# A bounds limit on the row gathers of a two-stage mixture-of-experts kernel, with four small clears per stage

## The reference

```
x = x + cross_attention(norm(x), ctx, wq, wk, wv, wo)        # own keys beside 1024 context rows
x = x + moe0(norm(x))    # 8 experts, 2 of them per token, inner width 256
x = x + memory_attention(norm(x), ctx, mask)
x = x + moe1(norm(x))    # 32 experts, 8 of them per token, inner width 192
moe: out[t] = sum over chosen experts e of w[t, e] * (silu(x[t] @ wgate[e]) * (x[t] @ wup[e])) @ wdown[e]
```

## Time and profile before

| what | value |
|---|---|
| median of 3 runs | 943.73 us (940.0 to 945.9) |
| the profiled execution, its own time | 939.34 us |
| its span | 937.6 us |
| TensorE / VectorE / ScalarE / GpSimd busy | 85% / 60% / 55% / 46% of the span |
| packets of q1 / q0, share of 16 DMA engines | 30.5% / 24.4% |
| bytes moved by DMA | 143.74 MB |
| moe0, from its first gather to its last scatter | about 282 to 383 us |
| moe1, likewise | about 575 to 912 us |

### The profile page before, as it was taken

The page is one execution under the profiler, slowest core; times in us unless marked ns, Lnnn a source line. Parts: engine busy times, 40 slices in busy tenths (PEclk is TensorE's granted clock), DMA queues, the critical chain, the costliest instruction groups (busy, mean ns, idle before and its releaser), DMA issues.

```text
span 937.6 us, 19263 instructions
## 1 busy us (share of the span) xinstructions
PE 796.3 (85%) x5266; PEld 437.7 (47%) x5267; DVE 559.9 (60%) x1596; ACT 516.6 (55%) x780; POOL 433.0 (46%) x355
## 2 busy tenths in 40 slices
PE   4999999999848999966888735999889899999995
PEld 2444455555425544433443414555555455555552
DVE  5553445555564555685676625576557575667475
ACT  6533234455445776333544523786777787778760
POOL 3882000200014676130075662467776666667862
PEclk9999999999968999998899876999999999999998
DMA  8562200201116696790120102898899897998777
GB/s 287 180 217 98 77 34 23 46 24 35 34 26 207 181 253 147 213 315 7 53 69 26 48 24 67 219 261 251 202 253 262 234 303 192 250 223 260 143 112 276
DMA packets 85842, 143.74 MB, mean 153 GB/s; under 512 B 19462, under 2 KB 36102, under 8 KB 85793
## 3 DMA queue, kind: packets, MB, share of 16 engines
q1 hardware_dynamic: 58880, 93.49, 30.5%
q0 software_dynamic: 24320, 49.45, 24.4%
q10 hardware_dynamic: 2592, 0.19, 0.2%
HBM read 106.25 MB, written 41.28 MB: 157 GB/s over the span
## 4 chain that ended last, share of the span: by engine, by line
PE 49%; issue 13%; DMA 12%; DVE 11%; ACT 6%; DVEq 2%; ACTq 2%; another core or an unknown queue 2%; POOL 1%; SPq 1%; POOLq 0%
PE pst L194 38%; PE pst L1368 4%; DMA mid<-moe_normalised_rows,row_no 3%; DMA x_rows<-mid,row_no 2%; PE pst L515 2%; DMA big<-in_L_ffn_wo_dram 2%; DMA xT<-moe_normalised_rows,row_no 2%; PE pst L1341 2%; DVE big L1247 1%; ACT mid L1431 1%; DMA x_rows<-xT,row_no 1%; PE pst L1423 1%; DVE mid L1520 1%; ACT big L1240 1%
## 5 line engine op out<-in xcount | busy, mean ns | idle before, releaser
L194 PE MATMUL pst<-big,mid 128*128 (+1 forms) x1392 | 272.1, 346 | 19.4 <-ACT mid L1431 13.1
L1056 POOL DMA_INDIRECT moe_tokens_of_experts<-token_no,small x70 | 73.3, 1047 | 271.3 <-DVE small L1141 253.7
L194 PEld LDWEIGHTS pst<-big,mid 128*128 128x128 f16 x1392 | 132.9, 98 | 122.1 <-issue 29.0
L1368 PE MATMUL pst<-big,mid 128*128 x520 | 128.9, 380 | 0.1
L1431 ACT ACTIVATE mid<-pst 128x1024 f16<-128x1024 f16 x100 | 102.5, 1025 | 29.7 <-PE pst L1341 19.9
L1622 POOL DMA_INDIRECT x_rows<-mid,row_no x48 | 90.9, 1894 | 48.8 <-DMA x_rows<-xT,row_no 22.5
L1622 POOL DMA_INDIRECT x_rows<-xT,row_no x46 | 87.7, 1906 | 52.3 <-DMA x_rows<-mid,row_no 20.9
L1520 DVE SCALAR_TENSOR_TENSOR mid<-pst,small,mid 128x192 f32<-128x192 f32 (+1 forms) x100 | 42.7, 427 | 106.6 <-ACT mid L1437 87.2
L194 PE MATMUL pst<-ctxN,mid 128*128 128x512 f16 x384 | 92.5, 399 | 3.1 <-ACT mid L647 3.1
L1245 DVE TENSOR_TENSOR big<-big (+2 forms) x40 | 74.6, 1864 | 3.7 <-issue 0.2
L1612 POOL DMA_INDIRECT mid<-moe_normalised_rows,row_no x52 | 54.9, 1055 | 46.1 <-DVE row_no L1503 22.1
(11 more groups left out here) (234 smaller groups left out, 1273.8 us busy)
## 6 DMA issues: line engine op xcount, KB each, us to landing
big<-in_L_ffn_w_gate_dram SPq DMA_DIRECT2D x32, 768.0 KB
big<-in_L_ffn_wi_dram SPq DMA_DIRECT2D x8, 1024.0 KB
big<-in_L_ffn_w_down_dram SPq DMA_DIRECT2D x32, 256.0 KB
big<-in_L_ffn_w_down_dram SPq DMA_DIRECT2D x64, 128.0 KB
moe_normalised_rows<-xn SPq DMA_DIRECT2D x18, 256.0 KB, 2.0
mid<-in_ctx_dram SPq DMA_DIRECT2D x16, 256.0 KB, 4.9
big<-in_ctx_turned_dram SPq DMA_DIRECT2D x16, 256.0 KB, 5.2
x_rows<-big SPq DMA_DIRECT2D x16, 256.0 KB, 3.8
```

What stands on the lines that cost most here:

```text
L194: last = nc.tensor.matmul(dst, stationary(a, c), moving(b, c), start=(k == 0), stop=(k == 3 * len(parts) - 1))
L1056: nc.gpsimd.indirect_dma_start(out=self.tab_d[:, :], out_offset=bass.IndirectOffsetOnAxis(ap=self.addr[j % 2][:, k:k + 1], axis=0), in_=to ...
L1368: last = nc.tensor.matmul(bank(6 + p), hT[:, k, :], self.d[:, s, h, c, :], start=(q == 0), stop=(q == len(seq) - 1))
```

## The change

Two edits. The gather gets the same bound as the scatter: an index above `NT * P - 1` is passed over, and the buffer keeps what it held in that partition. Since a buffer then may hold bits that no gather wrote, the weight columns of all four buffers are cleared once per stage by VectorE, between the two parts that compute the tables. The spare rows are still written to DRAM, and the waits for them stay.

```
     dve.sem_inc(s, self.CR)
 self.dve_route(dve)
+for g in range(4):
+    nc.vector.memset(self.xg[g][:, 2 * D:].bitcast(F32), 0.0)
 self.dve_rows(dve)
...
 nc.gpsimd.indirect_dma_start(out=self.xg[g].bitcast(U32), out_offset=None, in_=self.rows_d[:, :],
-                             in_offset=bass.IndirectOffsetOnAxis(ap=self.gi[g], axis=0)).then_inc(self.xg_in[g], 16)
+                             in_offset=bass.IndirectOffsetOnAxis(ap=self.gi[g], axis=0), bounds_check=NT * P - 1,
+                             oob_is_err=False).then_inc(self.xg_in[g], 16)
```

## The result

The changed kernel takes 937.68 us in the median of 20 runs, the kernel before 939.64 in 20 runs beside them. The ratio of the runs is 0.9944, with a 95% interval of 0.9918 to 0.997: 2.8 to 7.7 us faster, 5.3 in the middle. The two medians differ by 2.0 us, the means of the runs that lie within 1.5% of the fastest by 3.9. The profiled execution happened to be the slowest of its 20 (946.28 us), so its length says nothing; what it is good for are its rows.

The account below looks back on a forecast made before the run. TensorE in moe1 was taken to run near its floor, delayed by gathers queued behind other packets. Relief -4.5, bound +1 and clears +0.7 sum to -2.8 us, from 943.73 to 941 us; range 931 to 956.

Parts of the forecast that it names:

- The floor and the late gathers: TensorE in moe1: 3.65 us a tile when nothing is late; ten late gathers cost at most 12.5 us directly.
- Landing follows the queue, not a transfer's own rows: DMA queues in moe1: scatters of 128 and 5 rows land alike, 6.87 and 6.89 us, waiting for what is queued ahead.
- The relief in engine time: DMA engines, both stages: dropped rows save 3.10 to 4.51 us per MB, worth -4.5 us at the end.
- The bound: GpSimd's gathers: a bound costs 0.1 us each, within 0 to 0.61, adding 1 us at the end.
- The clears: VectorE before line 1326: four clears cost 0.35 us per stage, +0.7 us in all.
- Full relief: Rival: DMA queue limits moe1 and relief counts in full, -13 us, so 930.5 us; chance 0.21.
- The dear bound: Rival: the bound costs GpSimd all of 0.61 us per gather, +13.9 us, about 957 us; chance 0.19.
- the bound drops nothing: Rival on the gather: rows still move, only costs stay, 945.5 us; 0.10 together with relief only on the wrong engines.
- a dropped row costs an engine as much: Other form of the no-change rival: dropped gather rows save no engine time, +1.7 us, 945.5 us; in the same 0.10.
- The rule of the Trainium skill about consecutive partitions: DMA engines take consecutive partitions, so low ones keep all rows: gain near 0, 945 us; within the shared 0.10.

Follow-up runs that it names:

- wide_bound: Changed kernel plus floors of 1 under four waits, gather bound raised so no row is dropped, clears taken out: 941.28 us, 0.9972 of the kernel before.
- no_rows: Changed kernel plus floors of 1 under four waits, gather bound lowered to 0, all rows but row 0 left out: 934.32 us, 0.9894 of the kernel before.
- control: Kernel before with a floor of 1 under four waits computed from a loaded expert index: 0.9973 on the first chip, 1.0004 on the third.
- half_rows: Changed kernel plus floors of 1 under four waits, gather bound lowered to 511, tokens 512 to 1023 not gathered: 940.44 us, 0.9972 of the kernel before.
- base_before: Kernel before with a floor of 1 under four waits, first chip: 919.52 us, 0.9973 of the kernel before.
- pair_before: Kernel before with a floor of 1 under four waits, third chip: 940.27 us, 1.0004 of the kernel before.

## Why the prediction was right

**The floor and the late gathers.** 12.5 us were named as the most that gathers could cost TensorE in moe1. The ceiling measured by leaving all rows out is 7.0 us for both stages. Late gathers do cost TensorE time, and little of it, because other waits grow when they go (from 18.0 to 25.0 us in moe1), which the sum didn't foresee.

**Landing follows the queue, not a transfer's own rows.** This was read from a scatter with 5 rows and one with 128, and it carried the whole forecast. After the change the mid-stage landings are still 7.2 to 8.7 us, and with no rows at all one took 6.42. The scatter with 5 rows ends at 680.32 us and still has its 128 packets; the 123 of 8 bytes start from 683.4 to 685.0 us, amid the 832 packets that q1 starts from 679.6 to 684.9 and behind the gather before. So the reading of the two scatters was right. That step made the forecast small where "90% busy" invites a large one.

**The relief in engine time.** The ends were 3.10 and 4.51 us per MB. The lower one was the right price of a gathered row: 3.0 us per MB in the trace of the kernel before. Measured as relief it is 2.0 to 2.5. What this was taken to be worth at the end, -4.5 us, was too much. By the 0.25 us per MB between wide_bound and no_rows it is -1.5 us; by the measured totals of 2.0 to 3.9 us it is somewhat more. So the term was over-sized, up to threefold. Its outer end was given as -16 us, where the rival's own parts add up to -12 - 3 = -15.

**The bound.** Taken at 0.1 of a range of 0 to 0.61 us, measured 0.06 us. The choice to put the scatter's extra time down to its add is borne out: a bound alone is 0.06 of the 0.61. Its +1 us at the end can't be seen, wide_bound being at 0.9972 beside a control of 0.9973 and 1.0004 on other chips.

**The clears.** Taken at 0.35 us per stage; the trace has 0.16 in moe1 and 0.07 in moe0, because the four overlap. Over-sized too, so the errors cancel in part: -1.5 + 0.2 and a bound near 0 make -1.3 us, where -2.8 was forecast. The medians say -2.0 to -2.2, the means -2.6 to -3.9, the ratio of the 20 runs -5.3 with -2.8 at the edge of its interval. That there is a small gain is likely from the three comparisons together; whether it is 2 or 5 us stays open: runs of one kernel on one chip spread over 3 to 20 us.

**The level.** That 941 stands 3 us from 937.68 is partly chance. The sum was taken from the median of three runs, 943.73; twenty runs of the same kernel gave 939.64, and from there it would have been 936.8. The range of 931 to 956 also held every outcome in which nothing changes, so the time alone tests the mechanism little; no_rows, half_rows and wide_bound test it.

**The rivals.** Full relief, 930.5 us, is out: half_rows drops almost three times as many bytes and stays where wide_bound is. The dear bound, 957 us, is out by 0.06 us. That the bound drops nothing is out by q0's 43.39 MB, and that a dropped row costs an engine as much by q0's engine time, 15 us less. The rule of the Trainium skill about consecutive partitions ("DMA: Bandwidth & Descriptors", section "Why a DMA increments its semaphore by 16 and not by 1") would have made the gain near 0; spreading the spare slots gave no gain, so nothing shows that it held one back. No run here shows single engines, and that section doesn't speak of indirect DMAs.

## What to carry to other kernels

A DMA share of 0.9 was not a bound by itself here. Ask whether a transfer's landing follows its own bytes: compare two of very different size in the same stretch, as the scatters of 5 and 128 rows here, before pricing a saving in bytes. And price a saving by its ceiling: a run that leaves all rows out shows in one go what the last fifth of them can give, and which wait stands behind the one removed (here the copy behind ScalarE's weight splits).

## What the runs showed that was not expected

- Rows passed over by a bound leave the number of packets as it was, and what is left of them is nearly free. q0 has 24320 packets whether 49.45, 43.39 or 21.38 MB are moved; the packets under 512 bytes grow by 1397 for 2816 rows dropped, and by 6512 with nearly all 13056 dropped: one for every two rows, since a gather's packet holds two rows. Such a packet has 8 bytes and took 10 ns in the mean, where one of 4352 bytes took 210 (217 in the changed kernel). The 1397 are thus under 1 us of all 16 engines.

```profile
DMA packets 85841, 115.67 MB, mean 124 GB/s; under 512 B 25974, under 2 KB 42614, under 8 KB 85792
...
q0 software_dynamic: 24320, 21.38, 16.6%
```

- Adding rows into DRAM takes the engines more per MB than gathering rows does (6.7 against 3.0 us within the kernel before), and leaving the adds out saved 16.8 us where leaving out a like number of gathered bytes saved 7.0.
- Three chips ran the kernel before at 919.55, 940.58 and 944.89 us in the median, 2.8% apart; why is open. On the fast one the second stage starts 22.6 us earlier, at 554.52 us with its first gather in base_before, where it is 577.14 in pair_before.
